# Routing the second mixture inside the attention ahead of it, and splitting the next layer's self weights in that attention's last slots

## The reference, cut to what matters

```
x = x + jnp.tanh(g_xattn[2]) * _L2_xattn_ref(_layernorm(x, axis=-1), ctx_2048, ...)   # 16 heads, 256 queries, 256 keys
x = x + jnp.tanh(g_ffn[2]) * _L2_ffn_ref(_layernorm(x, axis=-1), ...)
x = x + jnp.tanh(g_xattn[3]) * _L3_xattn_ref(_layernorm(x, axis=-1), ctx_2048, ...)   # fp8, self and cross attention

def _L2_ffn_ref(x, router_logits, gating_einsum, linear, per_expert_scale, router_scale):
    ...
    logits = jnp.einsum('gsd,de->gse', router_input, router_logits.astype(dtype))
    ...
    _, choices = jax.lax.approx_max_k(logits32, k=k)
    ...
    sorted_xs = x_flat[xs_indices, :]
    ...
    activation = jax.nn.gelu(gate_out[:, 0, :]) * gate_out[:, 1, :]
    expert_outputs = jax.lax.ragged_dot(activation, linear.astype(dtype), group_sizes=tokens_per_expert)
    ...
    out = jnp.einsum('blkd,blk->bld', out, combine_weights, preferred_element_type=out.dtype)
```

## Time and profile before

| | |
|---|---|
| time, 3 runs | 1352.38, 1353.15, 1357.82 us; median 1353.15 |
| profiled execution | 1355.69 us, its span 1353.9 us |
| mean granted PE clock | 0.983 |
| busy in the span | PE 1256.9, DVE 963.5, ACT 817.2, POOL 672.1 us |
| end of l2x's products | 612.72 us from the span's start |
| first tile's rows turned | 618.66 us |
| tiles, and the first slots of l3x among the last of them | 618.66 to 735.50 us |

### The profile page before, as it was taken

How to read it: one execution, slowest core, us unless ns; L and a number is a source line. 1 busy time by engine, 2 the same in 40 slices (tenths; PEclk the granted TensorE clock), 3 DMA queues, 4 the chain that set the end, 5 groups by cost and what they waited for, 6 DMA issues and landing times.

```text
span 1353.9 us, 23541 instructions
## 1 busy us (share of the span) xinstructions
PE 1256.9 (93%) x7122; PEld 1053.3 (78%) x7122; DVE 963.5 (71%) x2457; ACT 817.2 (60%) x2057; POOL 672.1 (50%) x720
## 2 busy tenths in 40 slices
PE   6998999998799999998998799999999999999994
PEld 3556888886588888887886578888887888888784
DVE  7996665676786778744774677877778787877753
ACT  6954222333576767664644577777777777776363
POOL 1111555553343444442534366567768776764453
PEclk9999999999999999998999999999999999999897
DMA  6224555453231322237551992001311111033383
GB/s 237 86 102 120 155 167 175 124 164 108 78 106 47 119 72 92 95 109 267 180 184 48 322 335 67 1 1 32 121 60 32 40 55 32 32 104 124 102 304 112
DMA packets 90139, 159.62 MB, mean 118 GB/s; under 512 B 9324, under 2 KB 50953, under 8 KB 89515
## 3 DMA queue, kind: packets, MB, share of 16 engines
q1 hardware_dynamic: 82811, 144.55, 32.4%
q0 software_dynamic: 6640, 12.67, 2.8%
q10 hardware_dynamic: 576, 1.05, 0.2%
HBM read 103.86 MB, written 58.17 MB: 120 GB/s over the span
## 4 chain that ended last, share of the span: by engine, by line
PE 65%; DVE 13%; issue 7%; POOL 6%; ACT 5%; DMA 4%; POOLq 0%; SPq 0%; ACTq 0%; DVEq 0%
PE ps L1620 10%; PE ps L1752 8%; PE ps L1725 8%; PE ps L1703 7%; PE ps L1770 6%; PE ps L1634 5%; PE ps L1735 4%; PE ps L1453 4%; PE ps L1978 3%; PE ps L1714 3%; POOL urs L1157 2%; PE ps L1989 1%; DVE usum L3257 1%; ACT probs L2476 1%; DVE uve L3258 1%
## 5 line engine op out<-in xcount | busy, mean ns | idle before, releaser
L1164 POOL TENSOR_TENSOR probs<-probs,prec 128x512 f32<-128x512 f32 x192 | 202.7, 1056 | 287.6 <-DVE prec L3293 287.5
L2476 ACT ACTIVATE probs<-ps,nmax 128x256 f32<-128x256 f32 x384 | 179.1, 473 | 186.0 <-DVE nmax L3286 120.3
L1725 PE MATMUL ps<-k_feat,q_feat 128*128 128x256 f32 x768 | 197.9, 380 | 3.0 <-ACT q_feat L2466 2.2
L1752 PE MATMUL ps<-probs_t,v_tok 128*128 128x256 f32 x768 | 198.6, 381 | 0.2 <-ACT ob L2495 0.2
L1157 POOL TENSOR_TENSOR urs<-uve,neg_half 128x4 f32<-128x4 f32 x136 | 137.4, 1010 | 47.6 <-DVE uve L3258 36.8
L1725 PEld LDWEIGHTS ps<-k_feat,q_feat 128*128 128x128 f32 x768 | 136.4, 190 | 17.9 <-issue 4.9
L1752 PEld LDWEIGHTS ps<-probs_t,v_tok 128*128 128x128 f32 x768 | 131.5, 191 | 10.6 <-issue 0.6
L1735 PE MATMUL ps<-ident,probs 128*128 128x128 f32 x768 | 116.4, 274 | 16.1 <-ACT probs_t L2485 13.7
L1735 PEld LDWEIGHTS ps<-ident,probs 128*128 128x128 f32 x768 | 92.3, 140 | 48.8 <-issue 22.2
L2485 ACT ACTIVATE probs_t<-ps 128x512 f32<-128x512 f32 x192 | 115.6, 602 | 2.2 <-PE ps L1735 2.2
L3286 DVE TENSOR_REDUCE nmax<-ps 128x2 f32<-128x512 f32 x128 | 87.1, 681 | 37.8 <-PE ps L1725 37.5
(11 more groups left out here) (489 smaller groups left out, 3411.4 us busy)
## 6 DMA issues: line engine op xcount, KB each, us to landing
rows_in<-zero_rows SPq DMA_DIRECT2D x3, 5200.0 KB, 34.5
mid_more_w<-in_l2f_w SPq DMA_DIRECT2D x14, 768.0 KB, 6.5
tile_w<-in_l3f_w SPq DMA_DIRECT2D x21, 385.5 KB, 7.3
mid_rows<-mid_zero SPq DMA_DIRECT2D x6, 1040.0 KB, 5.4
w<-in_l1f_w SPq DMA_DIRECT2D x24, 256.0 KB, 5.0
spread_w<-we_dram SPq DMA_DIRECT2D x16, 384.0 KB, 3.8
mid_w<-in_l2f_w SPq DMA_DIRECT2D x8, 768.0 KB, 6.0
kv_cross<-kv_out SPq DMA_DIRECT2D x20, 256.0 KB, 2.0
```

Of the source, the lines that this page charges most:

```text
L1164: pool.tensor_tensor(p3, p3, spread(prec[g % 3][:, :], [P, TB, S]), ALU.mult)\
L1725: mm = pe.matmul(ps[g % 2][:, j * S:(j + 1) * S], q_feat[:, h, j * P:(j + 1) * P], k_feat[:, kv, :], start=True, stop=True)
L1752: mm = pe.matmul(ps[6][:, 0:S], v_tok[:, tb, kv * P:(kv + 1) * P], probs_t[g % 2][:, tb, :], start=tb == 0, stop=tb == TB - 1)
L2476: ins = act_e.activation(probs[g % 4][:, j, :], ps[g % 2][:, j * S:(j + 1) * S], ACT.Exp, bias=nmax[g % 3][:, j:j + 1], **kw, accum_out=ps ...
```

## The change: what it does

- The routing of batches 0 and 1 moves 6 to 14 slots earlier in l2x (turns at t = 48 and 50, logits 52, ranks 54). That of batch 2 now lies within l2x (turn 58, logits 60, ranks 62) instead of beside tiles 0 to 9. Only batch 3 is routed beside tiles (turn at j = 1, logits 3, ranks 5).
- The scatters: one a slot at t = 56 to 63, four at t = 65, one a tile at j = 3 to 6. Before: two a slot at t = 63 to 66, two a tile at j = 4, 5, 7, 8.
- `mid_map(0)` is cut in three and stands in slots 57 to 59, not behind the attention; `mid_map(1)` beside tiles 6 to 8, not 10.
- `high_self` goes to slots 57 to 64, `low_self` to slots 58 to 65.
- SP loads the first 8 tiles' rows ahead of three experts' weights, two later tiles' rows ahead of two later weights, and issues the loads of `mid_got` after tile 25's rows, ahead of later weights, not after tile 26's.
- Beside the tiles, `mid_add` and moments for l3x stand at j = 20, 21 (before: 19, 20), and `part_shift` ahead of `mid_prod` at j = 21, 22 (before: behind it at 20, 21).
- In l3x, for t = 0 to 2, DVE norms before it takes the maxima; `mid_add` and moments of batches 2 and 3 stand at t = 6, 7 (before: 3, 4), and what follows them 1 to 3 slots later than it stood.
- Buffers and PSUM banks are placed anew to allow this.

The diff, cut to its core:

```diff
-MID_LOGITS_BANK = (3, 5, 4)
+MID_LOGITS_BANK, MID_RANKS_BANK = (3, 2, 4), (2, 3, 5)
...
# SP
                         ("proj_ready", L2X.projection(2, "q", 3), (0,)), ("raw_ready", len(L2X.normed), (3,)),
-                        ("turn_ready", len(L2X.normed), (1,)), ("s_ready", L2X.total, (2, 4, 5, 6))):
+                        ("turn_ready", len(L2X.normed), (1,)), ("s_ready", L2X.total, (2,))):
...
                 for j in range(MID_RING):
                     rows(j)
+                for e in (4, 5, 6):
+                    fixed_weights(e)
...
-                later(MID_SETS)
-                later(MID_SETS + 1)
                 sp.wait_ge(*mid_at("placed", 16 * CHOICES * NT))
-                for j in range(first_b, first_b + 5):
-                    rows(j)
+                for i in range(2):
+                    rows(first_b + i)
+                for i in range(2):
+                    later(MID_SETS + i)
+                    rows(first_b + 2 + i)
...
                     load_mid_got(b)
+                rows(MID_ALL - 4)
+                for i in range(MID_SETS + 5, sum(MID_LATER) - 2):
+                    later(i)
...
# POOL, l2x slots
-                if 63 <= t < 67:
-                    mid_scatter(2)
+                if t == 65:
+                    pool.wait_ge(*mid_at("places", 3))
+                if 56 <= t < 64:
+                    mid_scatter(1)
+                if t == 65:
+                    pool.wait_ge(*mid_at("placed", 16 * CHOICES * TB * 2))
+                    mid_scatter(4)
...
# POOL, tiles
-                if j in (4, 5, 7, 8):
-                    mid_scatter(2)
+                if j == 3:
+                    pool.wait_ge(*mid_at("places", 4))
+                if 3 <= j < 7:
+                    mid_scatter(1)
...
# PE, l2x slots
-                if t == 57:
-                    pe.wait_ge(at["l2x"]["raw_ready"], len(L2X.normed))
-                    for b in range(2):
-                        turn_part(SECOND_LN, b, h_mid, quantised, (SECOND_LN - 1) * B + b + 1, ps[2 + b])
-                if t == 59:
+                if t in (48, 50, 58):
+                    b = (48, 50, 58).index(t)
+                    raw_taken((27, 28, 31)[b])
+                    turn_part(SECOND_LN, b, h_mid, quantised, (SECOND_LN - 1) * B + b + 1, ps[(3, 2, 3)[b]])
+                if t == 52:
+                    raw_taken(29)
                     mid_logits(0)
-                if t == 61:
-                    pe.wait_ge(at["l2x"]["turn_out"], len(L2X.normed))
+                if t == 54:
+                    raw_taken(30)
                     mid_ranks(0)
+                if t == 60:
+                    pe.wait_ge(*mid_at("places", 1))
+                    mid_logits(1)
+                if t == 62:
+                    mid_ranks(1)
...
# ACT, l2x slots
-                if t in (54, 55, 57):
-                    centre_part(SECOND_LN, (54, 55, 57).index(t), h_mid)
-                if t == 58:
-                    for b in range(2):
-                        second_copy(b, ps[2 + b])
-                if t == 61:
-                    mid_exp(0)
+                if t in (43, 45, 57):
+                    centre_part(SECOND_LN, (43, 45, 57).index(t), h_mid)
+                if t in (49, 51, 59):
+                    b = (49, 51, 59).index(t)
+                    second_copy(b, ps[(3, 2, 3)[b]])
+                if t in (54, 62):
+                    mid_exp((t - 54) // 8)
+                if 57 <= t < 65:
+                    high_self(t - 57)
...
# DVE, l2x slots
+                if t in (53, 61):
+                    mid_best_two((t - 53) // 8)
+                    mid_masks((t - 53) // 8)
+                if t in (55, 63):
+                    mid_marked((t - 55) // 8)
+                    mid_places((t - 55) // 8)
+                if 57 <= t < 60:
+                    next(first_map)
+                if 58 <= t < 66:
+                    low_self(t - 58)
...
# DVE, behind l2x
             v.sem_inc(layer_done, 1)
-            mid_map(0)
             part_moments(SECOND_LN, 3)
...
# DVE, attention slots
+                    if not f.biased and 0 <= t < 3:
+                        for u in f.normed_at(t - f.turn_lag + 1):
+                            normalise(u)
                     for g in f.heads_at(t):
                         maxima(g)
...
# DVE, l3x slots
-                if t in (3, 4):
-                    mid_add(t - 1)
-                    part_moments(LAST_LN, t - 1)
-                if t in (5, 6):
-                    part_shift(LAST_LN, t - 3)
+                if t in (7, 8):
+                    part_shift(LAST_LN, t - 5)
+                if t in (6, 7):
+                    mid_add(t - 4)
+                    part_moments(LAST_LN, t - 4)
...
# DVE, tiles
             for j in range(MID_ALL):
+                if j in (21, 22):
+                    part_shift(LAST_LN, j - 21)
                 mid_prod(j)
...
-                if j == 10:
-                    mid_map(1)
-                if 12 <= j < 20:
-                    low_self(j - 12)
-                if j in (20, 21):
-                    part_shift(LAST_LN, j - 20)
-                if j in (19, 20):
-                    mid_add(j - 19)
-                    part_moments(LAST_LN, j - 19)
+                if 6 <= j < 9:
+                    next(second_map)
+                if j in (20, 21):
+                    mid_add(j - 20)
+                    part_moments(LAST_LN, j - 20)
```

More of the change, by code:

```diff
@@ L386, in build @@
             mid_to = sb("mid_to", [P, MID_ALL], U32, where=a)
+            mid_best = sb("mid_best", [P, NT, MID], where=a)
+            mid_other = sb("mid_other", [P, NT, MID], where=a)
         mid_y = [front(f"mid_y{i}", 92 + i, [P, D]) for i in range(4)]
@@ L390, in build @@
         mid_more_front = [front(f"mid_more_w{i}", 32 + 6 * (i - 2), [P, MID_W]) for i in (2, 3)]
-        mid_got_front = [front(f"mid_got{b}", 80 + 4 * b, [P, TB, CHOICES, D]) for b in range(2)]
+        mid_got = [front(f"mid_got{b}", kb, [P, TB, CHOICES, D]) for b, kb in enumerate((80, 84, 44, 40))]
+        h_late_last = [front(f"h_late_last{i}", 44 + 2 * i, [P, TB, D]) for i in range(2)]
         w_high, w_low = ({n: sb(f"w{n}_{part}", shape, F32R) for n, shape in wshapes} for part in ("high", "low"))
@@ L569, in build @@
             mid_x = [sb(f"mid_x{i}", [P, ROW], where=a) for i in range(MID_RING)]
-        with ExitStack() as a:
-            sb("mid_lg_hold", [P, 68 * 256], where=a)
-            mid_lg = sb("mid_lg", [P, 4, MID], where=a)
-            mid_best = sb("mid_best", [P, NT, MID], where=a)
-            mid_other = sb("mid_other", [P, NT, MID], where=a)
-        mid_got = mid_got_front + [near(f"mid_got{b}", kb, [P, TB, CHOICES, D]) for b, kb in ((2, 72), (3, 76))]
-        h_late_last = [near(f"h_late_last{i}", 80 - 2 * i, [P, TB, D]) for i in range(2)]
         ps = [ctx.enter_context(nc.psum_tensor(f"ps{i}", [P, HALF], F32)) for i in range(8)]
@@ L1025, in mid_tiles @@
                     rows(j)
-                later(MID_SETS)
-                later(MID_SETS + 1)
                 sp.wait_ge(*mid_at("placed", 16 * CHOICES * NT))
-                for j in range(first_b, first_b + 5):
-                    rows(j)
+                for i in range(2):
[3 more added lines that the diff above has]
+                    rows(first_b + 2 + i)
                 more = registers(1)
                 experts_of, blocks = experts_of + more[0], blocks + more[1]
-                for i in range(5):
+                for i in range(3):
                     later(MID_SETS + 2 + i)
-                    rows(first_b + 5 + i)
-                for j in range(first_b + 10, MID_ALL - 3):
+                    rows(first_b + 4 + i)
+                for j in range(first_b + 7, MID_ALL - 4):
                     rows(j)
@@ L1840, in mid_ranks @@
                 pe.wait_ge(*mid_at("masks", part + 1))
-                bank = ps[5][:, MID_RANKS_AT[part]:MID_RANKS_AT[part] + (nt + 1) * MID]
+                bank = ps[MID_RANKS_BANK[part]][:, MID_RANKS_AT[part]:MID_RANKS_AT[part] + (nt + 1) * MID]
                 r = bank.rearrange("p (t e) -> p t e", e=MID)
@@ L3339, in attention @@
                         mean_square(u)
+                    if not f.biased and 0 <= t < 3:
+                        for u in f.normed_at(t - f.turn_lag + 1):
+                            normalise(u)
                     for g in f.heads_at(t):
                         maxima(g)
-                    for u in f.normed_at(t - f.turn_lag + 1):
-                        normalise(u)
+                    if f.biased or not 0 <= t < 3:
+                        for u in f.normed_at(t - f.turn_lag + 1):
+                            normalise(u)
                     if f.fp8:
```

99 lines of the change are left out of this document (46 added, 53 removed).

## The result

The changed kernel takes 1344.8 us (median of 4 runs, 1343.2 to 1345.7) where the one before takes 1354.0 beside it (4 runs): a ratio of 0.9922, with a 95% interval of 0.9904 to 0.9939. The forecast was faster, to 1339.4; the time lies in the range, and the gain is about two thirds of the 13.8 us of the sum.

The account below looks back on a forecast made before the run. PE was taken to bound the kernel, with few, long waits in three places. Terms 7.4 + 3.9 − 2.1 + 3.0 − 4.9 + 1.0 + 5.5 = 13.8 us, from 1353.15 to 1339.4; range 1332 to 1349.

Parts of the forecast that it names:

- A: Between l2x's attention and the first tiles: the wait for rows goes and mid_map(0) leaves, gaining 7.4 us.
- B: Tiles 2 to 15: less routing and no wait for tile 14's rows, gaining 3.9 us; 2.1 paid in the attention.
- C: Wait around tile 22: a later add and weights no longer queued ahead of the load cover it, gaining 3.0 us.
- D: Splits in l2x's last slots: queued ahead of work PE waits for, stalling about every second slot, losing 4.9 us.
- E: Start of l3x: norming first gains 1.0 us net, mid_add and moments leaving slots 3 and 4 gain 5.5; 6.5 together.
- Two times 2.6, and 0.3 for the later turns: l3x slots 3 and 4: mid_add and moments leaving save 2.6 us a slot, 5.5 in all (3 to 7).
- the attention gives it back: l2x's last slots: ACT's pieces stall in full, DVE's splits meet POOL's normalise; D 13.3, time 1347.8 us; chance 0.19.
- The slower case: Start of l3x: norming first makes PE wait 3.8 us in four slots, with lower clock; 1361.6 us; chance 0.09.
- The rival on the chain of C: Around tile 22 the chain stays, and tile 13's weights are late: C 0, B 2.5 less, 1344.9 us; chance 0.12.

Follow-up runs that it names:

- e1: Changed kernel with the splits of the self weights on ACT and DVE beside tiles again (tiles 11 to 18, 12 to 19): 1342.3 us, ratio 0.9914.
- e10: Changed kernel with DVE's mid_add and moments at tiles 19 and 20 and shifts behind mid_prod again, SP's order as changed: 1340.0 us, single run.
- e2: Changed kernel with DVE's splits alone beside tiles again (12 to 19), ACT's left in slots 57 to 64: 1342.1 us, ratio 0.9926.
- e9: Changed kernel with ACT's centring of batches 0 and 1 one slot later, at 44 and 46 of l2x: 1345.4 us, single run.
- e3: Changed kernel with the maxima ahead of the norming in all slots of l3x again: 1346.5 us, ratio 0.9956.
- e8: Changed kernel with splits beside tiles and the rows of tiles 8 to 11 each ahead of a later weight in SP's queue: 1341.1 us, ratio 0.9904.
- e4: Changed kernel with mid_add and moments of the last two batches at slots 3 and 4 of l3x again, followers as before: 1346.8 us, ratio 0.9952.
- e5: Changed kernel with ACT centring the last batch for layer 3 at slot 9 of l3x, not 8: 1344.4 us, ratio 0.9929.
- e6: Changed kernel with POOL's low halves of the output weights three slots later in l3x, 9 to 19: 1342.2 us, ratio 0.9912.

## Why the prediction was right, and where it was off

- **What bounds it** was read rightly: three waits in three places, and all went. Heads 0 to 44 of l2x and the stage from gates 24 to head 0 of l3x did not move.
- **A**, 7.6 for 7.4. DVE's chain behind the attention (finish, moments, root, shift, `mid_prod`) was sized well: `mid_act` of tile 0 was done at 625.11, 4.7 us behind PE's last product, where 4.9 was forecast. But PE did not wait for it. One wait of 0.56 us for `mid_feat` and PE's own work filled the 5.6 us.
- **B**, 4.2 for 3.9. No weight came late; without the 0.5 charged for that it would have been 4.4. The queue of weights was a real danger elsewhere: with tiles 5 us earlier it held up tile 8 (e1).
- **C**, 3.5 for 3.0: right in size, wrong in cause. "The add now comes one tile later (2.89 us)" was named as half of the cover. With the shift it costs 1.4 us (e10). The load could be issued 3.3 us sooner, and that did the work. The size came out by luck: a loss that was named as a gain, against a gain that was larger than forecast.
- **D**, −7.5 for −4.9. The mechanism held: splits ahead of `probs_t`, a stall in every second slot. The splits are 5.0 of it, 3.9 on ACT and 1.1 on DVE (e1, e2), for 4.9. What the step left out was slots 43 to 46, where I let batches 0 and 1 move for nothing: head 44 to 57 is 5.6 us longer, and less an estimated 3.8 of the routing's own products that is 1.8 of stalls, 1.2 of them waits for `probs_t`. A shift by one slot gives 1.0 back (e9). That leaves 0.7; e1 has a wait of 0.62 us for `probs_t` in slot 58, beside batch 2's routing, that was not there before.
- **E** is the term that was mis-sized, 3.6 for 6.5, in its second half. The norming went as forecast, down to the wait in slot 2 (3.75 for 3.8), and was worth 1.6 (e3) where I had 1.0. For the clock behind that wait I charged 1.5 us; by the place of head 4 it cost 1.6 here, 0 in e10 and 2.9 in e8, so that this figure was met by luck. The shortfall of E is no luck: in the seven runs of the changed code for l3x, head 0 to 19 is 2.8 to 4.9 us shorter than before. "Two times 2.6, and 0.3 for the later turns" failed. It took what leaves slots 3 and 4 as gain and the new slots as free, since fewer units are normed there. They were not free: POOL's output weights begin in slot 6 and hold DVE up, and ACT's centring and output weights stood in one slot. The move gained 5.9 us up to head 8, gave 5.8 back up to head 13, and is worth 0.2 to 1.1 (e4). What all of the giving back is made of stays open (e5, e6).
- The rival *the attention gives it back* was right in part: D went from 4.9 to 7.5, less than a third of the way to its 13.3. The slower case did not come; there was one gap of 3.8 us, in slot 2, not four. The rival on the chain of C has the measured time nearly to the tenth (1344.9 for 1344.8), and nothing of it came true: C gained 3.5 and no weight was late.

## What to carry to other kernels

When work is moved out of a place that waits, list what every engine does in the new place, one engine at a time, before it is counted as free. A piece put at the end of a slot delays the first thing of the next slot on its engine, so look for that one's play, not for idle time. And when a stage starts earlier, look next at the transfer queue that feeds it: the rows a tile needs should not stand behind weights that are needed later.
